# Feature rows loaded first, the first layer's gate and up weights with the routing stage, small setup loads on SyncE

## The reference

```python
mod = (_silu(L0_c) @ L0_wmod).reshape(16, 6, 1, -1)
sa, ca, ga, sb, cb, gb = (mod[:, i] for i in range(6))
h = _layernorm(x) * (1 + ca) + sa
x = x + ga * _L0_attn_ref(h, w_qkv, b_qkv, w_fc, b_fc)   # rope, softmax
h = _layernorm(x) * (1 + cb) + sb
x = x + gb * _L0_ffn_ref(h, ...)    # route to 8 of 64 experts: silu(x@Wg.T) * (x@Wu.T) @ Wd.T
mod = (_silu(L1_c) @ L1_wmod).reshape(16, 6, 1, -1)
h = _layernorm(x) * (1 + ca) + sa
x = x + ga * _L1_attn_ref(h, ...)   # state updated over the sequence
h = _layernorm(x) * (1 + cb) + sb
x = x + gb * _L1_ffn_ref(h, ...)
```

## Time and profile before

| | us |
|---|---|
| median of 3 executions | 1897.21 (1897.1 to 1898.57) |
| profiled execution, its own time | 1902.71 |
| its span | 1900.9 |
| attention with the setup | 0 to 385.3 |
| routing | 390.85 to 479 |
| experts, from its first instruction | 483.6 to the end |

### The profile page before, as it was taken

How to read it: one execution, slowest core, us unless ns; L and a number is a source line. 1 busy time by engine, 2 the same in 40 slices (tenths; PEclk the granted TensorE clock), 3 DMA queues, 4 the chain that set the end, 5 groups by cost and what they waited for, 6 DMA issues and landing times.

```text
span 1900.9 us, 25463 instructions
## 1 busy us (share of the span) xinstructions
PE 1675.3 (88%) x7212; PEld 1044.0 (55%) x7212; DVE 1384.9 (73%) x2654; ACT 791.3 (42%) x1487; POOL 668.1 (35%) x607
## 2 busy tenths in 40 slices
PE   4789889851899998999999999999998999999999
PEld 2455555441665655656556566565565555555555
DVE  6677777558676696897987979979789678544444
ACT  2466766721433323424334243352433643433333
POOL 0011111100000392691955928639378077000000
PEclk9888998955999999999999999999999999999999
DMA  6653444010677777666666666666664111111110
GB/s 204 228 143 107 114 134 112 25 64 0 199 222 220 211 249 206 188 203 188 204 191 183 194 186 200 196 186 206 180 189 128 40 45 53 42 51 55 50 48 29
DMA packets 168252, 269.56 MB, mean 142 GB/s; under 512 B 23261, under 2 KB 61494, under 8 KB 164958
## 3 DMA queue, kind: packets, MB, share of 16 engines
q1 hardware_dynamic: 164679, 266.67, 46.8%
q10 hardware_dynamic: 1440, 1.10, 0.2%
q0 software_dynamic: 2048, 0.79, 0.2%
HBM read 233.85 MB, written 34.62 MB: 141 GB/s over the span
## 4 chain that ended last, share of the span: by engine, by line
PE 33%; DVE 13%; POOL 12%; issue 10%; DMA 4%; ACT 2%; SPq 1%; DVEq 0%; POOLq 0%; ACTq 0%
PE psum L1508 10%; POOL e_prod L1878 8%; PE psum L1401 6%; PE psum L1402 5%; PE psum L1403 5%; PE psum L1410 4%; DVE psum L1809 3%; POOL e_phi L1878 3%; DMA rw<-rw_fm 3%; DVE e_y L1690 2%; DVE e_hm L1812 2%; PE psum L1447 1%; DMA e_ring<-w_split 1%; DVE e_state L1764 1%; DVE e_vbar L1690 1%
## 5 line engine op out<-in xcount | busy, mean ns | idle before, releaser
L1633 ACT ACTIVATE e_gu<-psum 128x512 f32<-128x512 f32 (+1 forms) x368 | 219.3, 598 | 597.2 <-DVE e_hm L1812 316.3
L1401 PE MATMUL psum<-e_hhi,e_ring 128*128 128x512 f32 x704 | 432.7, 615 | 25.4 <-DMA e_ring<-w_split 7.8
L1410 PE MATMUL psum<-e_hm,w_d 128*128 128x512 f32 (+1 forms) x736 | 382.3, 601 | 15.3 <-DVE e_hm L1812 7.5
L1878 POOL TENSOR_TENSOR e_prod<-e_state,e_phi 128x512 f32<-128x512 f32 x256 | 353.5, 1420 | 2.4 <-POOL e_phi L1878 1.7
L1809 DVE TENSOR_TENSOR psum<-psum,rw 128x512 f32<-128x512 f32 x352 | 243.9, 693 | 121.4 <-PE psum L1403 95.4
L1846 DVE TENSOR_TENSOR e_hm<-psum,rw 128x512 f32<-128x512 f32 x256 | 174.7, 689 | 175.4 <-ACT psum L1658 174.5
L1402 PE MATMUL psum<-e_hhi,e_ring 128*128 128x512 f32 x704 | 279.6, 397 | 0.0
L1403 PE MATMUL psum<-e_hlo,e_ring 128*128 128x512 f32 x704 | 279.4, 397 | 0.0
L1812 DVE TENSOR_TENSOR e_hm<-psum,e_gu 128x512 f32<-128x512 f32 x352 | 243.5, 692 | 37.1 <-ACT e_gu L1633 12.9
L1508 PE MATMUL psum<-e_hm,w_gu 128*128 128x512 f32 x512 | 262.2, 597 | 6.6 <-DVE w_d L1827 5.4
L1658 ACT ACTIVATE psum<-psum 128x512 f32<-128x512 f32 x256 | 148.8, 582 | 251.5 <-PE psum L1403 236.7
(11 more groups left out here) (225 smaller groups left out, 2166.6 us busy)
## 6 DMA issues: line engine op xcount, KB each, us to landing
e_ring<-w_split SPq DMA_DIRECT2D x308, 256.0 KB, 3.9
rw<-rw_fm SPq DMA_DIRECT2D x192, 176.0 KB
qk_parts<-at_part SPq DMA_DIRECT2D x96, 192.0 KB, 2.8
rw<-gates_fm SPq DMA_DIRECT2D x72, 256.0 KB, 3.2
w_split<-e_ring SPq DMA_DIRECT2D x44, 256.0 KB, 3.2
rw<-rw_fm SPq DMA_DIRECT2D x64, 160.0 KB
at_qs<-qk_parts SPq DMA_DIRECT2D x16, 576.0 KB
at_ks<-qk_parts SPq DMA_DIRECT2D x16, 576.0 KB
```

The costliest lines, as they stand in the source:

```text
L1401: pe.matmul(out, w_hi, x_hi, start=first, stop=False)
L1410: mm = pe.matmul(ps[:, ACC, :], weights_at(T, WD + P * j, P)[0:rows(j), :], hm[0:rows(j), slot(j), :], start=(j == 0), stop=(j == HT - 1))
L1633: a(act_g[0:r, j % 2, :], ps[0:r, GB[j % 2], :], ACT.Silu).then_inc(silu_done, 1)
L1878: ins = tt(out[:, at], x[:, at], y[:, at], op)
```

## The change

The load of `x_fm` moves from behind iteration -2 to the end of the setup's loads on SP. The loads of `wg` and `wu` move from behind iterations 0 and 1 to the routing block, between the gate tables and the down weights. Six small loads move from ACT (behind Silu) to SP (ahead of the second part of `x_tm`), and layer 1's half of `wmod` goes ahead of ACT's wait for Silu's input. Several semaphores are merged into three, with the counts shifted to fit: `products_done` counts PE's three results, `act_done` ACT's Silu and two Sqrts, `filled` POOL's two memsets and DVE's second one.

```diff
     def sync(self, sp):
...
-        sp.dma_start(T["ident"][:], A["ident"]).then_inc(self.w_loaded, 16)
+        for dst, src in ((T["ident"][:], A["ident"]), (T["w_v"][:], A["w_v"]), (T["w_fc"][:], A["w_fc"]),
+                         (T["bv_col"][:], A["b_v"]), (T["bfc_col"][:], A["b_fc"]), (T["ident_bf"][:], A["ident_bf"]),
+                         (T["bo_col"][:], A["b_o"])):
+            sp.dma_start(dst, src).then_inc(self.w_loaded, 16)
         sp.dma_start(T["x_tm"][:, first:], A["x_tm"][:, first:]).then_inc(self.x_in[1], 16)
+        sp.dma_start(T["x_fm"][:], A["x_fm"]).then_inc(T["x_fm_in"], 16)
 
     def sync_late(self, sp, n):
         T, A = self.T, self.A
-        if n == -2:
-            sp.dma_start(T["x_fm"][:], A["x_fm"]).then_inc(T["x_fm_in"], 16)
-        if n == 0:
-            sp.dma_start(T["w_gu"][:, WG:WU], A["wg"]).then_inc(T["ffn0_loaded"], 16)
-        if n == 1:
-            sp.dma_start(T["w_gu"][:, WU:WD], A["wu"]).then_inc(T["ffn0_loaded"], 16)
         if n == 2:
...
     def scalar(self, act):
...
         act.dma_start(self.rot[:], A["rot"]).then_inc(self.w_in_done, 16)
+        act.dma_start(self.wmod[:, 1, :], A["wmod"][:, 1, :]).then_inc(self.wmod_in[1], 16)
         act.wait_ge(self.wmod_in[0], 32)
-        nc.scalar.activation(self.cs[:], self.c_fm[:], ACT.Silu).then_inc(self.silu_done, 1)
-        for dst, src in ((T["w_v"][:], A["w_v"]), (T["w_fc"][:], A["w_fc"]), (T["bv_col"][:], A["b_v"]),
-                         (T["bfc_col"][:], A["b_fc"]), (T["ident_bf"][:], A["ident_bf"]), (T["bo_col"][:], A["b_o"])):
-            act.dma_start(dst, src).then_inc(self.w_loaded, 16)
-        act.dma_start(self.wmod[:, 1, :], A["wmod"][:, 1, :]).then_inc(self.wmod_in[1], 16)
+        nc.scalar.activation(self.cs[:], self.c_fm[:], ACT.Silu).then_inc(self.act_done, 1)
         self.root(act, 0)
...
     def rstd(self, dve, part):
...
-        dve.wait_ge(self.std_ready, part + 1)
+        dve.wait_ge(self.act_done, part + 2)
...
     def modulation(self, dve, l):
...
-        dve.wait_ge(self.mod_done, l + 1)
+        dve.wait_ge(self.products_done, 1 + 2 * l)
...
             su.scalar(act)
-            act.wait_ge(filled, 2)
+            act.wait_ge(filled, 3)
...
             sp.dma_start(gate_b[:], A["gate_b"]).then_inc(loaded, 16)
 
             routed = ROUTED_TILES * D
+            sp.dma_start(T["w_gu"][:, WG:WU], A["wg"]).then_inc(T["ffn0_loaded"], 16)
+            sp.dma_start(T["w_gu"][:, WU:WD], A["wu"]).then_inc(T["ffn0_loaded"], 16)
             sp.dma_start(T["w_d"][:, 0:routed], A["wd"]).then_inc(T["ffn0_loaded"], 16)
```

More of the change, by code:

```diff
@@ L83, in __init__ @@
         self.w_loaded = sem("su_w_loaded")
-        self.silu_done = sem("su_silu_done")
-        self.mod_done = sem("su_mod_done")
-        self.bias_done = sem("su_bias_done")
+        self.products_done = sem("su_products_done")
         self.var_ready = sem("su_var_ready")
-        self.std_ready = sem("su_std_ready")
+        self.act_done = sem("su_act_done")
         self.step = sem("su_step")
@@ L91, in __init__ @@
         self.rot_ready = sem("su_rot_ready")
-        self.one_set = sem("su_one_set")
         self.n = 0
@@ L117, in sync_late, with gpsimd @@
                 sp.dma_start(T[name][:], A[name]).then_inc(T["ffn0_loaded"], 16)
-    def gpsimd(self, pool):
-        pool.memset(self.one[:], 1.0).then_inc(self.one_set, 1)
-        pool.memset(self.T["eps"][:], LN_EPS).then_inc(self.one_set, 1)
+    def gpsimd(self, pool, filled):
+        pool.memset(self.one[:], 1.0).then_inc(filled, 1)
+        pool.memset(self.T["eps"][:], LN_EPS).then_inc(filled, 1)
     def root(self, act, part):
@@ L125, in root @@
         act.wait_ge(self.var_ready, part + 1)
-        self.nc.scalar.activation(self.dm[:, at], self.var[:, at], ACT.Sqrt).then_inc(self.std_ready, 1)
+        self.nc.scalar.activation(self.dm[:, at], self.var[:, at], ACT.Sqrt).then_inc(self.act_done, 1)
     def scalar(self, act):
@@ L148, in mods, with tensor_bias @@
                            start=True, stop=True)
-        mm.then_inc(self.mod_done, 1)
+        mm.then_inc(self.products_done, 1)
     def tensor(self, pe):
-        pe.wait_ge(self.silu_done, 1)
+        pe.wait_ge(self.act_done, 1)
         self.mods(pe, 0)
         pe.wait_ge(self.w_loaded, 16 * W_LOADS)
-    def tensor_bias(self, pe):
+    def tensor_bias(self, pe, filled):
         pe.wait_ge(self.rot_ready, 1)
-        pe.wait_ge(self.one_set, 2)
+        pe.wait_ge(filled, 3)
         for c in range(2):
@@ L161, in tensor_bias @@
                            self.one[:], start=True, stop=True)
-        mm.then_inc(self.bias_done, 1)
+        mm.then_inc(self.products_done, 1)
     def done(self, dve, ins, wait=True):
@@ L235, in vector_bias @@
         nc, T = self.nc, self.T
-        dve.wait_ge(self.bias_done, 1)
+        dve.wait_ge(self.products_done, 2)
         nc.vector.tensor_copy(T["bq_col"][:], T["psum"][:, BIAS_BANK, 0:1])
@@ L491, in late @@
                 if n == -3:
-                    su.tensor_bias(pe)
+                    su.tensor_bias(pe, filled)
                 if n == -2:
@@ L580, in late @@
                     su.vector_late(dve)
-            nc.vector.memset(v1[:], 0.0).then_inc(filled, 1)
-            dve.wait_ge(filled, 1)
+            su.done(dve, nc.vector.memset(v1[:], 0.0))
             nc.vector.memset(v1[:, :, :, :, DEPTH], 1.0).then_inc(filled, 1)
@@ L702, in iteration @@
                     nc.gpsimd.tensor_tensor(cols, cols, upd[:], ALU.add).then_inc(x_added, 1)
-            su.gpsimd(pool)
+            su.gpsimd(pool, filled)
             pool.wait_ge(T["x_fm_in"], 16 * (BUFS + 1))
```

## The result

Run on the same chip, in turns, the changed kernel takes 1885.19 us in the median (1882.19 to 1888.51, four executions) and the kernel before 1897.27. The ratio is 0.9935, with a 95% interval of 0.9918 to 0.9952: a gain of 12.1 us, where 15.1 had been forecast (a ratio of 0.9920). The time lies 3.1 us above the forecast and inside its range. The ratios and intervals are those of the record; they are not exactly the quotients of the two medians given beside them and differ from these by up to 0.3%. The profiled execution took 1888.51, with a span of 1886.7, against 1900.9 before: 14.2 us less. Two profiled executions more have spans of 1882.1 and 1886.5.

A forecast was written before the change was run, and what follows sets the result against it. PE stalls in iterations 1 and 2 for small DMAs behind `wg` and `wu`, plus late setup and first stack, were taken as the bound. 4.1 - 0.4 + 0.6 + 4.2 + 6.6 = 15.1 us gave 1882.1, range 1878 to 1888.5.

The forecast's parts named there:

- Setup, 4.1 forecast: Setup: ACT's table load and the small loads come sooner, so ACT's h starts 4.1 us earlier; bounds 1.5 and 4.6.
- That rival: Setup: small loads late all the same on SP, seven issues in a row; setup gains only 1.5 us, 1885; 8%.
- `x_fm` at -0.4: After the setup: first write of parts queues behind early `x_fm` on SP; 0.4 us lost, up to 1.4.
- the first stack at +0.6: First scores: stack comes in unhindered, scores lie ready before DVE's first maximum; 0.6 us gained, bounds 0 and 0.7.
- `wg` out of iteration 1, 4.2 forecast: Iteration 1: small DMA lands at 56.4, not 61.0, ACT's table load next late; 4.2 us gained, bounds 2.5 and 4.9.
- the 19.5 that the prediction named: Iteration 1: its stretch in the changed kernel's profile was to be near 19.5 us.
- `wu` out of iteration 2, 6.6 forecast: Iteration 2: 27.43 us becomes 20.5 to 21.34, stall and half-clock stretch gone; 6.6 us gained, bounds 5.0 and 6.9.
- Later iterations, allowed 2 us either way: Iterations 3 and later: untouched, but one can take 21.34 us against a mean of 20.5; 2 us allowed either way.
- Routing, nothing forecast: Routing: 8.8 MB of weights load in 23 us, far ahead of first use; no effect, bounds 0 and 1 us lost.
- The slower rival, routing starved of instructions: Routing: instruction fetches late by 5.1 us each; four or more, 1902 or slower, 3%; one to three, 5%.
- The rule weighed ahead: DMA engines: they alternate between queues packet by packet, so a 12 KB transfer would soon get its turn despite large loads.
- the first rival: Iterations 1 and 2: large loads do not cause the stalls; only setup and first stack gain, 4.3 us, 1893; 4%.

The follow-up runs named there:

- the repeats: The changed kernel itself, unaltered, measured on two later occasions: 1885.02 us (ratio 0.9924 to the kernel before) and 1883.70 us (0.9910).
- `x_fm` back: Changed kernel with only the `x_fm` load put back behind iteration -2: 1886.89 us, ratio 0.9920 to the kernel before.
- `wg` back: Changed kernel with only the `wg` load put back behind iteration 0: 1890.63 us, ratio 0.9945 to the kernel before.
- the setup alone: Changed kernel with `x_fm`, `wg` and `wu` loads all put back, leaving only the setup's edit: 1892.77 us, ratio 0.9960 to the kernel before.
- `x_fm` alone: Kernel before with only the `x_fm` load moved to the end of the setup's loads: 1902.17 us, ratio 1.0020.
- the first of these kernels: Changed kernel plus eight unread matmuls where PE waits: 1887.23 us, ratio 0.9924 to the kernel before.
- the others: That kernel plus an unread matmul behind each head's scores from the third on in iteration 0, run twice: 1881.28 us (0.9911) and 1888.18 us (0.9933).

## Why the prediction was right, and where it was not

It was right in sign and in size. By spans of profiled executions, which is what its sum was made against, 15.1 us were forecast and 14.2, 18.8 and 14.4 measured. By medians it was 12.1 on the first occasion, 15.8 and 19.3 on the later ones; by the record's ratios 12.3, 14.4 and 17.1. That the total came so near is in part luck: two parts of the sum were wrong in opposite directions, as follows.

**Setup, 4.1 forecast, 4.4 measured** (4.3 and 4.8 in the repeats). Every step holds: table load at 6.30, the reciprocal at 9.32 behind DVE's rotation (8.92 and 0.47), the transposes at 10.28, h at 11.40 with DVE's product on the bias as what it waits for. The small loads were not late on SP: `bo_col` went out at 5.07, and nothing waits for it. That rival falls.

**`x_fm` at -0.4, the first stack at +0.6: together +0.2 forecast, 1.5 to 1.7 measured** (what projection 1 gained, 5.8 to 6.5 us, less the setup's gain). Two terms were mis-sized. The first write of parts comes at 18.47, no later than the shift of the setup gives (23.00 - 4.39 = 18.61), so the queue behind `x_fm` cost nothing. And the bound of 0.7 us for the stack was too low. It counted only DVE's way to its first maximum. The maxima moved from 41.15 to 35.67 us, 1.1 us more than the setup gives, and iteration 0 from 21.35 to 19.87. Before, DVE stood in iteration 0 three times: 0.75 us for PE's scores at that first maximum, 0.42 for them once more (42.86) and 0.22 for a cut of parts (44.37) which had itself waited 6.05 us for the writes of the sequence before (43.71). After, it does not stand at all, and these 1.39 us are most of the 1.48 that iteration 0 gained. `x_fm` back puts 0.8 us of it back into iteration 0 (20.66), with DVE's second and third wait (0.42 and 0.22). With single executions this split is rough.

**`wg` out of iteration 1, 4.2 forecast: this is the step that failed.** The stall's cause was right (`wg` back, 4.81 us), and the small DMA was no longer late. But the iteration gained -0.6, 3.3 and 1.5 us in the three traces, in two of them less than the lower bound of 2.5. The step asked which wait comes next (ACT's table load) and not how fast PE itself was. The granted clock of that stretch reads 1.00, and I took it at its word; the pairs in the same trace, 0.63 us apiece until 71.2 and 0.38 after, show half speed. The counts in the rows hinted at it: 127 matmuls take 18.89 us there, and in iteration 3 155 of them 19.38. In the kernel before, PE's work and its stall fill iteration 1 (18.89 and 4.86 of 23.87 us), and the pace changes 17.4 us after its start. With the change the iteration starts 6 us earlier and has no stall, so more of its work comes ahead of the change of pace, and what it takes depends on when that is: 24.43 us with the change at 73.6, 22.35 at 67.0, 20.53 at 62.5. With the weights moved alone, so that iteration 1 starts at 54.25, it gains 4.0 us: there the 4.2 of the forecast holds. The runs with added matmuls show the rest: with part of iteration 1 at full speed it takes 19.6, which is the 19.5 that the prediction named.

**`wu` out of iteration 2, 6.6 forecast: 8.5, 5.1 and 6.2 measured.** The mean is right and the bounds of 5.0 and 6.9 are exceeded once. Again the clock: the 18.94 us ran in fast pairs from 73.6 on, while in the other two slow pairs came in at 84.3 and 85.6, for some 7 us. The forecast took the iteration as between 20.5 and 21.3; it had no case without a slow stretch. That PE slows after the long stall is what the trace of before shows: pairs take 0.38 us up to 78.64, some 0.6 from 86.12 to 91.2, and 0.38 again from 91.65. The projection at 310.56 begins iteration 13 and not 12; the nine iterations and their mean of 20.5 are right.

Together the two iterations gained 7.8 to 8.4 us and not 10.8; together the steps ahead of them gained 5.8 to 6.5 and not 4.3. The forecast at projection 3 was 15.1, the measurement 13.6 to 14.9. The two errors cancelled in part.

**Later iterations, allowed 2 us either way.** From projection 3 to the gate weights it is 282.2, 284.9 and 281.5 us, against 285.75 before. From the first expert's h to the end it is 1419.0, 1412.9 and 1418.6, against 1416.3. Stages that the change doesn't touch thus came out shorter by 0.9 to 4.3 us in the attention, and between 2.6 longer and 3.4 shorter in the experts. The first is no gain of the change: with `wg` and `wu` still in iterations 0 and 1 the stretch to the gate weights takes as little (281.1 with the setup alone, 281.2 with `x_fm` alone), and over the traces of all runs it lies between 277.5 and 286.0. The trace of before is one of the long ones. The allowance was too small, and it left out the experts altogether. This is also why one trace's span can't settle a few microseconds: the kernel with half of `wg` put back has a stall of 4 us and a profiled span of 1876.6, below all three of the changed kernel, while its median is above.

**Routing, nothing forecast.** It takes 94.49, 94.08 and 94.97 us against 93.72. With only the setup changed, and no `wg` or `wu` in it, it takes 94.84; with the two loads in it and nothing else changed, 93.77. The loads cost nothing there that these runs can show. The loads were in 22 us after their start, where 23 had been worked out. The slower rival, routing starved of instructions, falls.

**The rule weighed ahead.** The small DMAs land late behind a load from another queue: 4.8 us of stall for each weight tensor put back, and with `x_fm` alone the last of the six small setup loads on ACT landed 11.7 us after its issue instead of 6.6. Yet the packets are mixed: in the kernel before the small DMA's data moved in the middle of `wg`'s, 4.4 us after its issue. The Trainium skill, "DMA: Bandwidth & Descriptors", section on queues, rings and completion order, says that each DMA engine goes round between the queues that have work, packet by packet. The mixed packets agree with that; the innocence of the large loads, which the prediction drew from it as the first rival, does not, and the runs decided for the row.

## What to carry to other kernels

A bulk load put "early, because its time is free" can cost whoever has a small transfer in flight on another queue: look for the smallest DMA that an engine waits for, and put the bulk where no such wait is (here a stage bound by vector work), with the small loads issued ahead of it. Before a stall is counted as a gain, take the length of like instructions on the engine that waited, near the stall and late in the kernel: if it runs at half pace there, the engine itself is late next, and the gain is bounded by its busy time. Split a forecast by stages and take more than one trace of the same kernel before explaining a stage's difference of a few microseconds.

## What the runs showed of the hardware that was not expected

**The clock column is blind at the start.** The granted clock reads 1.00 for the stretch 47.68 to 72.11, while pairs of score matmuls follow each other after 0.43 us there and after 0.22 from 73.6 on. In every profiled execution without added matmuls PE began at the slow pace and changed between 62 and 76 us. With matmuls added in PE's waits it ran fast from about 33 us on, fell back in iteration 0 where PE waits for DVE's maxima (the pairs at 40.80 in the first of these kernels, at 38.68 and 37.95 in the others), and was fast again from 67.9 us on in the first and from 63.2 and 61.6 in the others, with three fast microseconds before that (from 53.1 and 52.3).

**A small transfer waits for large ones on other queues, but not in proportion.** 12 KB from POOL: 4.8 us of wait on PE behind 2.97 MB, 4.0 behind 1.48 MB issued 0.7 us ahead, none behind 0.74 MB issued 3.3 us ahead, and 5.4 behind a stack load of 0.58 MB issued 0.1 us ahead. In the delayed cases whose packets are given above its data begin to move 3.7 to 4.4 us after the issue instead of 1.2, behind the whole `wg` amid the load and not after it. What sets this was not found.

**The spread of one kernel is wider than its first runs said.** The kernel before gave 1897.1 to 1898.6 in the first four executions and 1891.7 to 1910.3 in later ones, some 0.5% to either side of the middle.
